# First attention: three PSUM banks for the scores and two for the maxima, instead of two and three

## The reference

```python
q = jnp.einsum('bsd,hqd->bhsq', x, w_q)
k = jnp.einsum('bsd,hqd->bhsq', x, w_k)
v = jnp.einsum('bsd,hvd->bhsv', x, w_v)
scores = jnp.einsum('bhsq,bhtq->bhst', q, k)
masked = jnp.where(causal, -jnp.inf, scores)
weights = jax.nn.softmax(masked / jnp.sqrt(jnp.float32(dq)), axis=-1)
out = jnp.einsum('bhst,bhtv->bhsv', weights, v)
cat = out.transpose(0, 2, 1, 3).reshape(b, s, -1)
return jnp.einsum('bsf,df->bsd', cat, w_o)
```

## Time and profile before

| | |
|---|---|
| timed runs, median of 3 | 2751.97 us (2751.84 to 2753.37) |
| profiled execution | 2745.91 us, span 2744.2 us |
| TensorE busy | 2388.5 us (87% of the span) |
| VectorE busy | 1636.8 us (60%) |
| ScalarE busy | 1446.1 us (53%) |
| GpSimd busy | 965.5 us (35%) |
| granted TensorE clock, mean | 0.945 |
| first and last score of the first attention start at | 85.6 us, 1324.9 us |

### The profile page before, as it was taken

One profiled execution on the slowest core, in us unless ns is written; L12 is line 12 of the kernel. 1 busy time (PEld: TensorE's weight loads), 2 busy tenths in 40 slices (PEclk: granted clock), 3 DMA queues, 4 the chain that ended last, 5 costly groups with the idle time before them and its releaser, 6 DMA issues. The chain is left out here.

```text
span 2744.2 us, 45471 instructions
## 1 busy us (share of the span) xinstructions
PE 2388.5 (87%) x12594; PEld 1372.3 (50%) x12595; DVE 1636.8 (60%) x4291; ACT 1446.1 (53%) x3189; POOL 965.5 (35%) x1727
## 2 busy tenths in 40 slices
PE   4999999999999999999735899999998749999980
PEld 2555566555665556555512333333334626666650
DVE  5676664776467773676188777777773452222227
ACT  3566654666456663665257477777775412222222
POOL 0344433444345542444326122222222033333323
PEclk8999999999999999999968799999999869999995
DMA  3011110101001110111124111111111611111114
GB/s 103 17 28 29 25 44 15 29 22 41 24 19 29 29 44 14 29 26 28 32 97 194 40 35 34 35 35 35 35 34 58 218 51 44 46 44 46 46 55 163
DMA packets 134983, 135.01 MB, mean 49 GB/s; under 512 B 67840, under 2 KB 104448, under 8 KB 133120
## 3 DMA queue, kind: packets, MB, share of 16 engines
q1 hardware_dynamic: 125760, 109.58, 13.4%
q0 software_dynamic: 6912, 18.88, 2.1%
q10 hardware_dynamic: 2112, 4.19, 0.4%
HBM read 87.50 MB, written 33.82 MB: 44 GB/s over the span
## 5 line engine op out<-in xcount | busy, mean ns | idle before, releaser
L288 POOL TENSOR_TENSOR a_A<-a_A,a_P 128x512 f32<-128x512 f32 (+3 forms) x320 | 316.5, 989 | 289.8 <-PE a_O L594 279.0
L1229 ACT ACTIVATE b_P<-b_SC 128x512 f32<-128x512 f32 (+3 forms) x768 | 328.8, 497 | 163.0 <-PE b_SC L1332 161.4
L442 ACT ACTIVATE a_P<-a_SC 128x512 f32<-128x512 f32 (+3 forms) x640 | 292.0, 469 | 201.2 <-PE a_SC L577 194.9
L500 DVE CUSTOM_DVE_ANT_0 a_MX<-a_MX,a_causal 128x128 f32<-128x128 f32 (+3 forms) x512 | 248.5, 501 | 154.8 <-PE a_MX L646 149.3
L576 PE MATMUL a_SC<-a_QR,a_KR 128*128 128x512 f32 (+3 forms) x768 | 317.3, 417 | 4.6 <-DMA a_QS<-a_minusT 2.9
L1171 POOL TENSOR_SCALAR_AFFINE_SELECT b_P<-b_P 128x128 f32<-128x128 f32 x512 | 147.0, 294 | 443.0 <-ACT b_P L1229 433.6
L646 PE MATMUL a_MX<-a_KR,a_QR 128*128 128x512 f32 (+3 forms) x768 | 282.6, 377 | 17.5 <-DVE a_peak L500 14.3
L1279 DVE CUSTOM_DVE_ANT_0 b_MX<-b_MX,b_causal 128x128 f32<-128x128 f32 (+3 forms) x512 | 248.5, 498 | 80.3 <-PE b_MX L1381 78.1
L1381 PE MATMUL b_MX<-b_K,b_Q 96*128 96x512 bf16 (+3 forms) x768 | 251.7, 339 | 42.3 <-ACT b_Q L1240 14.0
L577 PE MATMUL a_SC<-a_QS,a_KS 65*128 65x512 f32 (+3 forms) x768 | 264.5, 348 | 0.0
L327 POOL TENSOR_SCALAR_AFFINE_SELECT a_P<-a_P 128x128 f32<-128x128 f32 x448 | 144.8, 329 | 339.7 <-ACT a_P L442 336.3
(11 more groups left out here) (258 smaller groups left out, 4083.5 us busy)
## 6 DMA issues: line engine op xcount, KB each, us to landing
a_inv<-inv_rows SPq DMA_DIRECT2D x128, 128.0 KB, 3.1
stack_rows<-p_stk SPq DMA_DIRECT2D x32, 480.0 KB, 2.7
a_W<-in_w_pair SPq DMA_DIRECT2D x34, 384.0 KB, 3.9
b_stk<-stack_rows SPq DMA_DIRECT2D x136, 96.0 KB, 2.1
W<-in_w SPq DMA_DIRECT2D x8, 1024.0 KB, 5.5
n_x<-in_x SPq DMA_DIRECT2D x4, 1024.0 KB, 9.5
a_xT<-hold SPq DMA_DIRECT2D x4, 1024.0 KB, 4.9
a_fold<-a_total SPq DMA_DIRECT2D x256, 1.0 KB, 2.0
```

Source lines behind the costliest of these rows:

```text
L288: eng.tensor_tensor(acc[h][c][:, a:], acc[h][c][:, a:], buffer(n, h)[:, a:], ALU.add).then_inc(added[h], 1)
L442: act.activation(buffer(n, h)[:, a:], SC[h][:, a:], ACT.Exp, scale=DH1 ** -0.5).then_inc(s["exp_done"], 1)
L500: dve.tensor_tensor_reduce(MX[c % MAX_BANKS1][:, 0:w], MX[c % MAX_BANKS1][:, 0:w], causal[:, BANK - w:], 1.0, 3 * NEG, ALU.add, ALU.max, p ...
L1229: act.activation(probs[k % RING2][:, a:], SC[k % SCORE_BANKS][:, a:], ACT.Exp, scale=DH2 ** -0.5).then_inc(s["exp_done"], 1)
```

## The change

The scores get a third bank and the maxima keep two, so that all eight banks stay in use (three others hold the context and the projections). Scores now take the bank by their number in the pair, (2n + h) modulo 3, where it was the head's. `exp_done` starts at 3, so a score waits for the exponential three scores back; every wait on it that others make is shifted by the same one and so still means what it did. `max_used` starts at 2, so a maximum waits for the reduction two maxima back.

```diff
-MAX_BANKS1 = 3
+SCORE_BANKS1, MAX_BANKS1 = 3, 2
...
-        SC = [ps(f"a_SC{h}", [P, BANK]) for h in range(2)]
+        SC = [ps(f"a_SC{i}", [P, BANK]) for i in range(SCORE_BANKS1)]
         MX = [ps(f"a_MX{i}", [P, BANK]) for i in range(MAX_BANKS1)]
...
-                eng.wait_ge(s["exp_done"], n2 * N2 + 2 * n + h + 3)
+                eng.wait_ge(s["exp_done"], n2 * N2 + 2 * n + h + 1 + SCORE_BANKS1)
...
-            act.sem_inc(s["exp_done"], 2)
+            act.sem_inc(s["exp_done"], SCORE_BANKS1)
...
-                            act.activation(buffer(n, h)[:, a:], SC[h][:, a:], ACT.Exp, scale=DH1 ** -0.5).then_inc(s["exp_done"], 1)
+                            act.activation(buffer(n, h)[:, a:], SC[(2 * n + h) % SCORE_BANKS1][:, a:], ACT.Exp, scale=DH1 ** -0.5).then_inc(s["exp_done"], 1)
...
                 pe.wait_ge(s["exp_done"], n2 * N2 + 2 * n + h + 1)
-                pe.matmul(SC[h][:, a:], KR[p][h][:, keys], QR[p][h][:, queries], start=True, stop=False)
-                pe.matmul(SC[h][:, a:], KS[p][h][:, keys], QS[p][h][:, queries], start=False,
+                bank = SC[(2 * n + h) % SCORE_BANKS1]
+                pe.matmul(bank[:, a:], KR[p][h][:, keys], QR[p][h][:, queries], start=True, stop=False)
+                pe.matmul(bank[:, a:], KS[p][h][:, keys], QS[p][h][:, queries], start=False,
                           stop=True).then_inc(s["scores_ready"], 1)
...
-                pe.wait_ge(s["exp_done"], n2 * N2 + 4 * g + 6)
+                pe.wait_ge(s["exp_done"], n2 * N2 + 4 * g + 4 + SCORE_BANKS1)
```

More of the change, by code:

```diff
@@ L322, in step @@
                             t = buffer(n, h)[:, a:a + P]
-                            pool.wait_ge(s["exp_done"], n2 * N2 + 2 * n + h + 3)
+                            pool.wait_ge(s["exp_done"], n2 * N2 + 2 * n + h + 1 + SCORE_BANKS1)
                             pool.sem_inc(s["due"], 1)
```

## The result

The changed kernel took 2810.0 us (median of 4 runs, 2805.4 to 2811.4), the kernel before 2752.2 (2751.8 to 2753.4). The ratio is 1.0219, 95% interval 1.0204 to 1.0233: slower by 58 us. The forecast was slower, 2800 in a range of 2786 to 2816. The profiled execution has a span of 2803.7 us, 59.5 more than before.

A forecast was written before the change was run, and what follows sets the result against it. TensorE was taken to bound the kernel, with 0.44 us of slack a step. Steps 42.8 us, bare pass 3 and edges 2 made 48 us, giving 2800 us on the timed median, in a range of 2786 to 2816.

The forecast's parts named there:

- TensorE is the bound, and its queue's order decides: Steady first attention: TensorE busy 35.89 of a 36.33 us step, so whatever makes its queue wait longer lengthens the kernel.
- The third score bank is worth 0: Score matmuls: waiting for the exponential three scores back instead of two gains 0, bounds 0 and -3 us.
- M2's delay is swallowed by M4's: Early step: the third maximum ends 0.94 us later, which vanishes in the fifth maximum's delay of 2.12 us.
- M4 waits for M2's reduction: Early step: the fifth maximum waits for the third's reduction, held by ScalarE's copies, and starts 2.12 us late.
- M7 costs 0.21 us: Slot 2 of a step: the eighth maximum waits for the sixth's bank, taking the delay from 1.17 to 1.38 us.
- Bare pass: Pair 0's maxima, run without scores: two banks cover less of each projection, costing 3 us (0 to 5).
- Edges: First and last steps with scores and three with the output projection: early maxima at other times, 2 us (0 to 4).
- The clock falls: Rival: more idle TensorE halves its clock, a projection taking 1.6 us more once a step, 50 us: 2850; chance 0.05.
- my other cases: Forecast (0.80), delay spreading through ScalarE (0.09), faster by the third score bank (0.03), no difference (0.03).
- one of my own signs of being wrong: First attention stage: a half clock inside it was listed among the signs that the prediction was wrong.
- my row: Profile at 743 to 747 us: TensorE busy only 2.01 of 4.00 us with the clock at 1.00, cited against the clock falling.
- The delay spreads: Rival: ScalarE gets slot 2's score 1.83 us late and the whole step follows, 62 us, 2814; chance 0.09.

The follow-up runs named there:

- M2 waiting alone: Kernel before, with only the third of a pair's 24 maxima waiting for the reduction two maxima back: 2749.5 us, ratio 1.0005.
- the run with M4 alone: Kernel before, with only the fifth of a pair's 24 maxima waiting for the reduction two maxima back: 2800.4 us, ratio 1.0196.
- the runs with M2 and M4, and M7 as well: Kernel before, with a pair's third and fifth maxima waiting for two back: 2796.3 us; with the eighth as well: 2809.3 us.

## Why the prediction was right, and where it was off

- *TensorE is the bound, and its queue's order decides.* Right: busy time stayed and waits were added one for one.
- *The third score bank is worth 0 (0 to -3 us).* Right: with two score banks the ratio is the same.
- *M2's delay is swallowed by M4's.* Right, shown by M2 waiting alone: step unchanged.
- *M4 waits for M2's reduction, which ScalarE's copies hold back.* Right in place and size: 2.13 us late (2.12), and 1.17 left behind M6. Moving the reduction ahead of the subtraction took M4's wait away.
- *M7 costs 0.21 us.* Mis-sized: 0.35. I had VectorE start 0.03 us behind the end of M5 in the trace; it was 0.19. The 0.03 was that of the reduction of M10, a TENSOR_REDUCE, and M5's is one with the mask. The kernel before shows both. A masked reduction, of M22 (no projection ahead of its matmul), starts 0.19 us behind the matmul's end at 1224.68:

```profile
1224.34 0.34 PE L646 MATMUL a_MX<-a_KR,a_QR 128*128 128x384 f32 x1
1224.87 0.57 DVE L500 CUSTOM_DVE_ANT_0 a_MX<-a_MX,a_causal 128x384 f32<-128x384 f32 x1 [1.27 <-PE a_MX L646]
```

  and a TENSOR_REDUCE, of M13 (its matmul right behind a projection), 0.04 us behind the end at 1211.36:

```profile
1209.25 1.88 PE L620 MATMUL a_PK<-hold,a_W 128*128 128x512 f32 x4
1210.57 0.79 PE L646 MATMUL a_MX<-a_KR,a_QR 128*128 128x512 f32 x1
1211.40 0.69 DVE L503 TENSOR_REDUCE a_peak<-a_MX 128x1 f32<-128x512 f32 x1 [0.84 <-PE a_MX L646]
```

  31 steps of 0.14 are 4.3 us.
- *Bare pass 3 us (0 to 5).* Mis-sized: the first score starts 5.7 us later (91.3, was 85.6):

```profile
L577 PE MATMUL a_SC<-a_QR,a_KR x768: 220/395/798, 91.3 to 1383.3; 128*128 128x512 f32 x128, 128*128 128x256 f32 x64
```

Two waits of it, and the projection between at half clock (it took 1.93 us before):

```profile
62.71 0.44 PE L647 MATMUL a_MX<-a_KR,a_QR 128*128 128x384 f32 x1 [0.44 <-DVE a_peak L500]
...
65.29 3.73 PE L621 MATMUL a_PK<-hold,a_W 128*128 128x512 f32 x4
...
71.91 0.50 PE L647 MATMUL a_MX<-a_KR,a_QR 128*128 128x512 f32 x1 [0.86 <-DVE a_peak L500]
```

  The projection alone has 1.8 of the 5.7 us. TensorE's list of waits has 5.5 us ahead of these maxima where it had 2.7, which makes 2.8 more; the 1.1 that is left is not divided.
- *Edges 2 us.* The steps with scores lost 52.7 us, 31 times 1.53 is 47.4. Of the other 5.3, 2.4 lie in the first and 3.3 in two of the steps with the output projection (the last distance has 0.8 more than the rest, the scores of the last pair take 0.9 less, and a few steps a little less): what I had put down to maxima standing at other times is mostly half clock.
- *The clock falls: 0.05.* As a case of once a step it didn't come, but my other cases left the clock at none, and that was wrong: a half clock inside the stage, one of my own signs of being wrong, is there. Stretches of the changed kernel at half, where the kernel before has one between 94 and 1300 us:

```profile
94.20:101.00 6.80, 5.40 (x9) 2.74 (x10) 2.97 (x10) 2.33 (x5) 0.88 (x3) 0.50 0.00 0
401.40:404.80 3.40, 3.40 (x6) 1.35 (x5) 1.01 (x5) 0.00 (x0) 0.67 (x2) 0.50 0.00 0
780.30:783.70 3.40, 3.40 (x10) 2.69 (x9) 0.00 (x0) 0.00 (x0) 0.00 (x0) 0.50 0.00 0
1114.80:1118.20 3.40, 3.40 (x9) 2.69 (x9) 0.00 (x0) 0.00 (x0) 0.00 (x0) 0.50 0.00 0
```

  The first two rows stand at waits of maxima. The last two come shortly after the start of an output projection that had itself waited 2.0 us. Each kernel has three such waits; in the kernel before the clock stayed at 1.00 behind two of them and was at half behind the first (from 423.5 us). One of the changed kernel's:

```profile
779.65 6.70 PE L657 MATMUL a_PV<-a_Wo,a_cat 128*128 128x256 f32 x22 [1.98 <-POOL a_cat L314]
```

  So my row was one instance of a thing that goes either way. Five such stretches of 3.4 us less the one of before are about 6 us.
- *The delay spreads.* It didn't: ScalarE got its score late by the 1.83 us forecast (1.84), and 0.40 us idle is left on it.

The sum with what was measured: 47.4 in steps, 5.3 at the edges, 5.7 in the bare pass, and 1.1 behind the last score, 59.5 us. I had 42.8, 2, 3 and 0. All four were low, and the edges and the bare pass lay above their own bounds of 4 and 5. The mechanism of the steps was right; that the range held the time was in part luck, because its upper end reached for the delay that spreads, which didn't come. The Trainium skill (TensorE: Matmul & The Clock Gate, "A second HAM failure mode: psum-queue depth-cycling") was nearer to the truth than I gave it: in the run with M4's waits of 2.0 us for a PSUM bank the clock went down and up again at 7 of the 31 waits, where the kernel before has no half clock at a maximum. But it didn't do so in every step, and at waits split into 0.7 and 1.3 us not at all.

What stays open: which of two equal waits of 2 us is followed by a half clock, what the 0.72 us a step consist of that two banks cost with the subtraction moved, and how the bare pass divides; it was not tried by itself.

## What to carry to other kernels

A buffer count is worth what the tightest consumer of it allows: look in the trace for each user at the distance from the release of the buffer one less to the start that needs it, and work the sum through to the place where the queues meet again, since a wait may swallow another. Here three of 24 users made the loss, and about half of it (0.81 of 1.53 us a step) hung on one instruction ahead of a reduction in VectorE's queue, which itself waited for a third engine, ScalarE. Try such a move in the kernel before as well: here it helped there too, and with the users spread it gained 27 us (2722.2 against 2749.4) with the banks left as they were. Take the time from a matmul's end to its reader's start from the same kind of reader. And where TensorE's idle times come near 2 us, count in some half clocks of 1.6 us each, or split or fill the waits.

## What the runs showed of the hardware that I had not expected

Granted clock: behind an idle time of 2.0 us TensorE's clock was 0.50 for 3.4 us in some of the steps and 1.00 in others of the same program, with the same instructions ahead: at 7 of 31 waits of 2.0 us in the run with M4 alone, and at 4 and 5 of 7 waits of 1.95 to 2.00 us in the runs with M2 and M4, and M7 as well. Where the idle time was split into 0.7 and 1.3 us with work between, no stretch at half stands at any of the 24 such waits of each of four runs (these two, the changed kernel, and two and two banks). Length alone doesn't decide it: in the changed kernel the stretch from 401.4 us stands at a wait of M4's of 1.28 us, and the wait ahead of that one was of 0.42 us.

VectorE: a masked reduction (L500) that waits for its matmul starts 0.19 us behind the end that the trace gives the matmul, a TENSOR_REDUCE (L503) 0.04 us, whether or not a projection stands ahead of the matmul.
